# Expert outputs scattered back by token and loaded plainly, with expert tiles of two 256-row halves

## The reference

```
x = x + window_attention(group_norm(x))          # shifted 8x8 windows, 8 heads, relative bias
t = x as 32768 tokens of 128 channels
t = t + banded_attention(layer_norm(t))          # 128-token windows, 4 heads, band of 32
n = layer_norm(t)
probs = softmax(n @ gate_w + gate_b)             # 8 experts
top2_vals, top2_idx = top_k(probs, 2)
t = t + sum over the two chosen experts e of  top2_val * (gelu(n @ W1[e] + b1[e]) @ W2[e] + b2[e])
```

## Time and profile before

| | us |
|---|---|
| median of three runs | 3094.0 |
| the three runs | 3090.27 to 3098.82 |
| span of the profiled execution (first to last instruction) | 3088.7 |
| median over that span | 5.3 |
| PE busy | 2544.2 (82%) |
| VectorE busy | 1965.5 (64%) |
| POOL busy | 1914.2 (62%) |
| ACT busy | 1865.7 (60%) |

### The profile page before, as it was taken

How to read it: one execution, slowest core, us unless ns; L and a number is a source line. 1 busy time by engine, 2 the same in 40 slices (tenths; PEclk the granted TensorE clock), 3 DMA queues, 4 the chain that set the end, 5 groups by cost and what they waited for, 6 DMA issues and landing times.

```text
span 3088.7 us, 77036 instructions
## 1 busy us (share of the span) xinstructions
PE 2544.2 (82%) x27338; PEld 1794.8 (58%) x27338; DVE 1965.5 (64%) x5091; ACT 1865.7 (60%) x3409; POOL 1914.2 (62%) x2270
## 2 busy tenths in 40 slices
PE   6898889989888899889988988899888887676830
PEld 3565655556666666666666666666665665554520
DVE  4577777777666666777676676767776765522222
ACT  3666656666767677677776677767777654432310
POOL 1335555555444444576666576666667878779986
PEclk9998888888999999899999999999999988788965
DMA  5223333334445454144333343434343434456743
GB/s 208 104 110 117 117 132 150 147 127 138 147 173 182 161 183 161 60 148 123 100 122 117 107 144 122 126 96 127 119 149 111 131 109 135 123 171 203 244 127 91
DMA packets 262427, 421.99 MB, mean 137 GB/s; under 512 B 41740, under 2 KB 141080, under 8 KB 261280
## 3 DMA queue, kind: packets, MB, share of 16 engines
q1 hardware_dynamic: 219232, 327.69, 31.2%
q0 software_dynamic: 32768, 67.17, 7.7%
q10 hardware_dynamic: 10048, 22.19, 2.2%
HBM read 198.26 MB, written 231.22 MB: 139 GB/s over the span
## 4 chain that ended last, share of the span: by engine, by line
PE 48%; POOL 17%; ACT 15%; issue 10%; DVE 7%; DMA 2%; ACTq 1%; SPq 1%; POOLq 0%; DVEq 0%
PE bank_m L834 7%; POOL yg L1233 7%; PE bank_m L827 4%; PE bank_to L761 4%; POOL x_sorted L1223 4%; PE bank_s L801 4%; PE bank_s L807 3%; PE bank_s L716 3%; ACT pt_sb_a L1051 2%; POOL xin L1243 2%; PE bank_to L770 2%; PE bank_s L729 2%; ACT L1178 2%; ACT v_a L1036 2%; PE bank_s L739 2%
## 5 line engine op out<-in xcount | busy, mean ns | idle before, releaser
L1223 POOL DMA_INDIRECT x_sorted<-xn_c,place_i x512 | 534.3, 1044 | 282.1 <-PE bank_s L700 109.2
L1233 POOL DMA_INDIRECT yg<-y_sorted,place_i x512 | 521.4, 1018 | 241.1 <-PE bank_to L783 107.5
L1216 POOL TENSOR_TENSOR s_sb_a<-s_sb_a,mx_a 128x512 f32<-128x512 f32 x256 | 267.8, 1046 | 587.7 <-DVE mx_a L1607 586.9
L1599 DVE TENSOR_TENSOR s_sb_a<-bank_s,bias_a 128x512 f32<-128x512 f32 x256 | 176.6, 690 | 355.3 <-PE bank_s L700 257.7
L827 PE MATMUL bank_m<-xe,wk_e 128*128 128x512 f32 x552 | 280.5, 634 | 37.7 <-ACT hid L1084 27.7
L834 PE MATMUL bank_m<-wk_e,hid 128*128 128x128 f32 x2208 | 283.3, 291 | 0.9 <-ACT hid L1084 0.9
L834 PEld LDWEIGHTS bank_m<-wk_e,hid 128*128 128x128 f32 x2208 | 277.7, 208 | 2.2 <-issue 1.9
L1216 POOL TENSOR_TENSOR s_sb_b<-s_sb_b,mx_b 128x512 f32<-128x512 f32 x256 | 269.7, 1054 | 11.5 <-DVE mx_b L1607 11.5
L761 PE MATMUL bank_to<-k_consts,p_sb_b 128*128 128x128 f32 x1024 | 179.0, 300 | 92.2 <-ACT pt_sb_a L1051 56.1
L1051 ACT ACTIVATE pt_sb_b<-bank_to 128x512 f32<-128x512 f32 x256 | 152.5, 596 | 146.4 <-PE bank_to L761 145.7
L1207 POOL TENSOR_TENSOR km_a<-qk_a,k_consts 128x128 f32<-128x128 f32 x512 | 215.7, 445 | 40.0 <-DVE qk_a L1451 35.4
(11 more groups left out here) (221 smaller groups left out, 6266.7 us busy)
## 6 DMA issues: line engine op xcount, KB each, us to landing
y_sorted<-t_back SPq DMA_DIRECT2D x192, 512.0 KB, 5.5
y_sorted<-yo SPq DMA_DIRECT2D x170, 256.0 KB
wk_e<-in_w_experts_dram SPq DMA_DIRECT2D x134, 321.0 KB
xs<-x_sorted SPq DMA_DIRECT2D x134, 256.0 KB
t_kept<-t SPq DMA_DIRECT2D x64, 256.0 KB
t_back<-t_kept SPq DMA_DIRECT2D x32, 512.0 KB
xin<-in_x_dram SPq DMA_DIRECT2D x128, 112.0 KB
x_res<-in_x_dram SPq DMA_DIRECT2D x256, 56.0 KB
```

What stands on the lines that cost most here:

```text
L1216: pool.tensor_tensor(s[:, :, :], s[:, :, :], m[:, :, None].to_broadcast(shape), ALU.subtract).then_inc(s_sub[w], 1)
L1223: pool.indirect_dma_start(out=x_sorted[group_of[d] % XSIDES].ap(), out_offset=bass.IndirectOffsetOnAxis(ap=place_i[:, d, n:n + 1], axis=0) ...
L1233: pool.indirect_dma_start(out=yg[:, c % 2, n, :], out_offset=None, in_=y_sorted[side].ap(), in_offset=bass.IndirectOffsetOnAxis(ap=place_i ...
L1599: tt(s_sb[0][:, :, :].rearrange("p (r h) n -> p r (h n)", h=2), scores, bias_a[:, kind, :, :].rearrange("p (r h) n -> p r (h n)", h=2), AL ...
```

## The change

The order of moving rows is turned round. Before, outputs are stored sorted and gathered by token. Afterwards POOL scatters each output tile to its tokens' rows (`scatter_back`, four indirect DMAs of 128 rows for a tile, into `y_tokens`), and an image's outputs are then read with one plain 1 MB load on SP (`bring_back`). For that, each sorted token row carries two more numbers, its home row and its first expert (`ROW_W` is 130 instead of 128); DVE writes them in `gate_choices` (three more instructions for an image) and works the target row out in `slots_back` (two more for a tile). Spare places get rows with targets of their own (input `spare`).

A tile of 512 rows becomes two halves of 256 (`SLOTS = 256`, `PART = 2`), each with its own place and its own expert's weights: two row loads and two weight loads for a tile, each with its own values read from the table. `hidden` is four matmuls of 256 columns instead of two of 512, `gelu` four of 256 instead of two. The surplus of a group falls from 7 tiles of 512 to 8 of 256. `plan()` then gives 152 tiles in 76 pairs, all of two tiles: 57 pairs with 114 tiles in passes 10 to 31, 6 in passes 32 and 33, and 13 with 26 tiles in the tail, where images 22 to 31 are summed. Two images may be summed in a pass from pass 24 on; pass 16 has no pair, passes 15, 17, 22, 23 and 28 have two.

POOL's rows stand at places written out by hand: `OUT_AT` for the 16 scatters of an image, `BACK_AT` for the 8 rows of the pair in each slot, as (step, k) with steps 8 and up in the next pass. The memsets between rows, the fills with zeros, `store_pair` and `gather` go away. `yo` has three buffers, and DVE waits before it writes one until its four rows have landed.

```diff
-SLOTS = 512
+SLOTS = 256
+PART = 2
+ROOM = PART * SLOTS
+HOME, FIRST, ROW_W = D, D + 1, D + 2
+YO, MOVES = 3, PART * SUB
+BACK_AT = (((4, 1), (4, 1), (4, 2), (4, 3), (4, 3), (5, 0), (5, 1), (5, 2)),
+           ((6, 1), (6, 2), (6, 3), (7, 1), (7, 2), (7, 3), (8, 0), (8, 1)),
+           ((9, 1), (9, 2), (9, 3), (10, 1), (10, 2), (11, 0), (11, 1), (11, 2)))
+OUT_AT = ((5, 0), (5, 2), (5, 3), (6, 0), (6, 1), (6, 2), (6, 3), (7, 0), (7, 1), (7, 2), (7, 3),
+          (8, 0), (8, 1), (8, 2), (8, 2), (8, 3))
-TWO_SUMS_FROM = 29
-PAIRS_PER_SUM = 2.5
+TWO_SUMS_FROM = 24
+PAIRS_TO_SUM = 3
...
@@ load_pair @@
-                row = eng.value_load(tiles[0:1, kth:kth + 1], min_val=0, max_val=BUFFER - SLOTS)
-                expert = eng.value_load(tiles[0:1, MAX_TILES + kth:MAX_TILES + kth + 1], min_val=0, max_val=E - 1)
-                rows = x_sorted[side].ap()[bass.ds(row, SLOTS), :].rearrange("(p j) d -> p (j d)", p=P)
-                eng.dma_start(xs_b[b], rows).then_inc(tile_in[b], 16)
-                weights = w_experts[bass.ds(expert, 1), :, :].rearrange("e p n -> (e p) n")
-                eng.dma_start(wk_b[b], weights).then_inc(tile_in[b], 16)
+                for h in range(PART):
+                    at = kth + h
+                    row = eng.value_load(tiles[0:1, at:at + 1], min_val=0, max_val=BUFFER - SLOTS)
+                    expert = eng.value_load(tiles[0:1, MAX_TILES + at:MAX_TILES + at + 1], min_val=0, max_val=E - 1)
+                    rows = x_sorted[side].ap()[bass.ds(row, SLOTS), :].rearrange("(p j) d -> p (j d)", p=P)
+                    eng.dma_start(xs_b[b][:, h, :, :].rearrange("p j w -> p (j w)"), rows).then_inc(tile_in[b], 16)
+                    weights = w_experts[bass.ds(expert, 1), :, :].rearrange("e p n -> (e p) n")
+                    eng.dma_start(wk_b[b][:, h, :], weights).then_inc(tile_in[b], 16)
...
@@ bring_back @@
+                after(sp, stored[home], 16 * IO_DMAS * y_uses(c))
+                tiles_landed(sp, last_tile[group_of[c]])
+                first = last_image[group_of[c] - 1] + 1 if group_of[c] else 0
+                at = TOP * (SPARE + TOKENS * (c - first))
+                rows = y_tokens[group_of[c]].ap()[at:at + TOP * TOKENS, :]
+                sp.dma_start(y_home[home].rearrange("p t n d -> p (t n d)"),
+                             rows.rearrange("(p r) d -> p (r d)", p=P)).then_inc(y_in[home], 16)
...
@@ hidden @@
-                    mm(banks[:, ch, :], w[:, P * ch:P * ch + P], xe[:, m, :], start=True, stop=True).then_inc(z_ready, 1)
+                    for h in range(PART):
+                        own = slice(SLOTS * h, SLOTS * h + SLOTS)
+                        last = mm(banks[:, ch, own], w[:, h, P * ch:P * ch + P], xe[:, m, own], start=True, stop=True)
+                    last.then_inc(z_ready, 1)
...
@@ gelu @@
-                    func(hid[:, CH * m + ch, :], banks[:, ch, :], ACT.Gelu,
-                         bias=w[:, B1_AT + ch:B1_AT + ch + 1]).then_inc(gelu_ready, 1)
+                    for h in range(PART):
+                        own = slice(SLOTS * h, SLOTS * h + SLOTS)
+                        last = func(hid[:, CH * m + ch, own], banks[:, ch, own], ACT.Gelu,
+                                    bias=w[:, h, B1_AT + ch:B1_AT + ch + 1])
+                    last.then_inc(gelu_ready, 1)
...
@@ GpSimd @@
-            def gather(c, n):
...
-            def apart():
...
+            def scatter_back(u, k):
+
+                _, q, _ = pairs[u].members[k // MOVES]
+                if k % MOVES == 0:
+                    pool.wait_ge(yo_ready, q + 1)
+                j = k % MOVES
+                pool.indirect_dma_start(out=y_tokens[pairs[u].group].ap(),
+                                        out_offset=bass.IndirectOffsetOnAxis(ap=back_to[:, q % YO, j:j + 1], axis=0),
+                                        in_=yo[:, q % YO, j, :], in_offset=None).then_inc(y_out[q % YO], 16)
...
@@ slots_back @@
-                after(dve, y_out[q % 2], 16 * (q // 2))
-                tt(yo[:, q % 2, :, :], banks[:, m, :].rearrange("p (j d) -> p j d", j=SUB),
-                   w[:, None, B2_AT:B2_AT + D].to_broadcast([P, SUB, D]), ALU.add).then_inc(yo_ready, 1)
+                after(dve, y_out[q % YO], 16 * MOVES * (q // YO))
+                for h in range(PART):
+                    stt(back_to[:, q % YO, SUB * h:SUB * h + SUB], rows[:, h, :, FIRST], w[:, h, OWN_AT:OWN_AT + 1],
+                        rows[:, h, :, HOME], ALU.not_equal, ALU.add)
...
```

More of the change, by code:

```diff
@@ L119, in shape_constants @@
     put("base", rows(REGION * e))
+    put("experts", rows(e))
+    put("home", TOP * (SPARE + TILES * ch[:, None] + np.arange(TILES)[None]))
     img = np.zeros((SIDE, SIDE), np.int32)
@@ L171, in plan @@
     for g, size in enumerate(GROUPS):
-        tiles = list(range(TOP * size * TOKENS // SLOTS + E - 1))
+        tiles = list(range(0, TOP * size * TOKENS // SLOTS + SURPLUS, PART))
         for k in range(0, len(tiles), 2):
@@ L499, in load_residual @@
                                      x_rolled[a, r, c0:c1, tiles, :]).then_inc(xr_in[h], 16)
-            def store_pair(u):
-                pair = pairs[u]
-                side, tiles = pair.group % YSIDES, table[pair.group % TABLES]
-                if pair.group >= YSIDES:
-                    sp.wait_ge(summed, SUM_STEPS * (last_image[pair.group - YSIDES] + 1))
-                else:
-                    sp.wait_ge(filled[side], 16 * FILLS)
-                for m, q, kth in pair.members:
-                    sp.wait_ge(yo_ready, q + 1)
-                    row = sp.value_load(tiles[0:1, kth:kth + 1], min_val=0, max_val=BUFFER - SLOTS)
-                    rows = y_sorted[side].ap()[bass.ds(row, SLOTS), :].rearrange("(p j) d -> p (j d)", p=P)
-                    sp.dma_start(rows, yo[:, q % 2, :, :].rearrange("p j d -> p (j d)")).then_inc(y_out[q % 2], 16)
             def spill(c, h):
@@ L565, in _ @@
                     load_residual(a, 1)
-                if before[2] is not None:
-                    store_pair(before[2])
                 if here[1] is not None:
@@ L1300, in _ @@
                     step(i, t)
-            for k in range(12, TOP * TILES):
-                scatter(IMAGES - 1, k)
-                apart()
-            for c in sums[PASSES - 1][1:]:
-                for k in range(12, TOP * TILES):
-                    gather(c, k)
-                    apart()
-            for c in range(first_tail_sum, IMAGES):
-                for k in range(TOP * TILES):
-                    gather(c, k)
-                    if c < IMAGES - UNPAUSED:
-                        apart()
+            for row, (t, _) in enumerate(OUT_AT):
+                if t >= TILES:
+                    scatter(IMAGES - 1, row)
+            for u in tail:
+                for k in range(MOVES * len(pairs[u].members)):
+                    scatter_back(u, k)
         @block.vector
@@ L1540, in tile_table @@
                 if g >= TABLES:
-                    for n in range(2):
-                        dve.wait_ge(y_out[n], 16 * ((last_tile[g - TABLES] + 1 - n) // 2))
+                    dve.wait_ge(yo_ready, last_tile[g - TABLES])
                 tt(seen[:, :], total, const("base", 1), ALU.subtract).then_inc(tabled, 1)
```

326 lines of the change are left out of this document (161 added, 165 removed).

## The result

The changed kernel takes 3171.98 us (median of four runs, 3165.45 to 3175.18) against 3092.14 us for the kernel before on the same chip: 1.0265 times as long, 95% interval 1.0222 to 1.0307. The forecast was 3054 with a range up to 3140. It is slower, and outside the range. The profiled span is 3172.9.

What follows compares the result with a forecast made beforehand. PE was taken to set the pace in passes 18 to 28, POOL in pass 32 and the tail. Span 3088.7 + 113 (passes 10 to 31) - 16 (pass 32) - 137 (tail) = 3048.7, so 3054 measured; range 2935 to 3140.

Steps and rivals of the forecast that it cites:

- POOL's crowd in steps 6, 7 and 0: Passes 10 to 31: added scatter-back rows make POOL the bound there, +7.3 a pass, +5.8 without sums, +145 in all.
- Up to step 5 PE hides them: Three-pair passes: PE's work covers POOL's rows up to step 5, but for 0.7 by which step 6's subtraction comes late.
- the 6 forecast for `gelu`: Passes 10 to 31: four `gelu` of 256 columns cost 0 to 0.27 a tile, +6 for 114 tiles, bounds 0 and 31.
- slower rival: POOL sets the whole pass and PE's clock falls while it waits: 10.8 in each of 21 passes, 3136; chance 0.17.
- first rival: Rows hidden behind PE's chain, POOL's step 7 results ready before PE needs them: 0.7 a pass, 2924; chance 0.18.
- Halves: Expert tiles: `hidden` as four narrower matmuls costs 0, bounds -0.1 to +0.47 a tile; `gelu` +6 for 114 tiles.
- narrow matmuls: Rival: each of four more `hidden` records a tile costs a 128-column one, +66, giving 3120; chance 0.04.
- VectorE and SP: Added vector instructions cost 0, about 30 in all if uncovered; `slots_back` wait 0, or 1 to 2 a pass; SP's loads 0.
- Pass 32: 40 rows without memsets and 8 subtractions on POOL: 71 instead of 87.4, -16.
- The tail: No gather, 13 pairs instead of 20, ACT's rounds 13.4: 214 instead of 351.5, -137, bounds 175 and 285.
- the rival of late loads: Tail: twice the weights come late, pairs at 19 us, tail 285, total 3125; chance 0.09.
- The rule that speaks against rows on POOL: VectorE blocks GpSimd's DMA descriptors, 620 ns growing to 3100; 120 more rows caught would cost 470 us, judged not borne out.

Runs made afterwards that it cites:

- tail_sp: Changed kernel with the loads of the tail's pairs issued by SP instead of ACT; 3130.99 us, 1.0150 of the kernel before.
- tiles_512: Changed kernel with the halves undone: tiles of 512 rows with one place and one expert; 3171.35 us, 1.0279 of the kernel before.
- keys_first: Changed kernel, all 40 rows kept, two moved from between step 6's subtraction and masked keys to behind the keys; 3142.14 us, 1.0184 of the kernel before.
- gelu_whole: spread2 with `gelu` unsplit, two instructions of 512 columns a tile; 2993.02 us, 0.9695 of the kernel before.
- one_row_moved: Changed kernel scattering back one of a tile's four rows in the passes, slot 1's first moved behind step 6's masked keys; 2997.10 us, 0.9732 of the kernel before.
- spread2: Changed kernel, its 40 rows a pass spread over other places, none between step 6's subtraction and keys; 2996.76 us, 0.9723 of the kernel before.
- best: spread2's places with tail_sp's loads on SP, the tail's first two pairs' loads ahead of a store; 2951.59 us, 0.9564 of the kernel before.
- spread: Changed kernel with the same 40 rows a pass spread over other places, five in step 5; 3011.46 us, 0.9742 of the kernel before.

## Why the prediction was wrong, point by point

On the span, 3172.9 instead of 3048.7, it missed by 124: 72 in passes 10 to 31, 4 in pass 32 and 48 in the tail.

**POOL's crowd in steps 6, 7 and 0: right in mechanism, nearly right in size.** Subtraction to subtraction took 14.0 in step 6 (forecast 13.6) and 12.7 in step 7 (13.3); keys for step 1 were ready 5.5 after step 0's (5.2). From step 6's subtraction to step 1's scores it is 32.3, just the forecast without its 0.7. That subtraction came 1.5 late rather than 0.7 (4.52 after the scores, 3.00 before the change). Steps 6, 7 and 0 grew by 8.0 a pass (29.0 to 37.0); 7.3 was forecast.

**"Up to step 5 PE hides them": this step failed.** The sum ended at step 1's scores and put steps 1 to 5 at nothing; they grew by 3.1. Step 1 has 1.4 of it: PE now waits 2.2 for the keys before it, and in pass 24 its clock is 0.60 instead of 0.83. This goes with the crowd. In the four versions that have it (after, tail_sp, tiles_512, keys_first) the mean wait before step 1 is 1.5 to 2.2, its clock 0.63 to 0.66 and its length 12.0 to 12.4; in all others, before included, there is no wait, the clock is 0.76 to 0.89 and the length 9.9 to 11.0. Steps 2 and 4 have 0.6, from `gelu`. Step 3 has 1.1, which doesn't go with the crowd (11.9 in tiles_512, 12.9 in gelu_whole) and whose cause is open; in tail_sp, with the same passes, it has 0.5. The passes gained 11.1 instead of 7.3, and the six without sums 7.7 instead of 5.8 (85.2 to 93.0 in passes 11 to 14): 15 x 3.8 + 6 x 1.9 = 68. Less the 6 forecast for `gelu`, that is 62 of the 72 by which passes 10 to 31 missed. (By `plan()` passes 27 and 31 sum no image either, so the forecast's 15 passes at 7.3 should have been 13, 3 us less.) The text had this as its slower rival, POOL setting the pass and the clock falling with it, at 10.8 a pass; the passes went that way. The fault was to take waits and their clock for two cases, with chances of their own. one_row_moved shows that they come together: take the wait away, and the step after it is 1.0 shorter, at a clock of 1.00 instead of 0.86.

**The place of a row wasn't in the sum.** It counted rows per interval at 1.28 each, and 1.5 once for the slower keys. One row ahead of the keys of step 7 is worth some 48 us without the crowd; eighteen rows at other places cost nothing that can be measured (one_row_moved against spread2, 0.9732 and 0.9723). The rows had the sign: before the change PE already waited 0.83 for these keys in pass 24, so nothing put ahead of them could be hidden, and the first rival's "ready before PE needs them" doesn't hold for them. The rival that the rows would be hidden was right in what PE's chain can bear, and wrong about the places they were put at.

**Halves: the products right, `gelu` low.** A tile's eight matmuls take 1.97 to 1.99 (four took 1.95), 246 to 249 ns a record where half of 488 is 244: so about 0, and narrow matmuls are no cost. Four `gelu` took 1.57, above the 1.53 bound, and the rest wasn't "mostly beside PE's other work": steps 2 and 4 show 0.3 each. By tiles_512 halves cost 1.4 to 2.1 a pass, 26 to 40 in all, against 6 with a bound of 31; only 0.6 of it is traced to `gelu`, and most of the rest lies in step 3, whose time varies without them.

**VectorE and SP: right on the path, VectorE's work too low.** In passes 18 to 27 PE's waits that are put down to VectorE come to 8.0 us, where passes 18 to 28 before had 8.4, and one wait of 2.2 to a tile's weights. But "about 30 in all" for the added instructions, were they uncovered, was far too low: 284 of the new ones in `slots_back` (L1580) alone took 133.9, half of them about 0.22 or less each and the longest 2.76.

**Pass 32:** 75.1 instead of 71, so -12 for -16.

**The tail: mis-sized, 262.9 instead of 214.** The end was right in sum, 35.2 from the last tile's output at 3137.75 to the end, but three images are summed there, 4.7 each, where the text had one and slower loads. Three terms were low. The first pair's copy comes 17.5 after the tail's start instead of 4.5, since its loads stand behind a store in SP's list, and SP issues them until 2922.7. In best, where they stand ahead of that store, the copy comes 8 earlier (14.3 instead of 22.3 after ACT's last gating instruction).

```profile
2909.96 3.16 SPq L575 DMA_DIRECT2D out_dram<-yg  x8
2914.80 0.37 SPq L521 DMA_DIRECT2D qk_a<-x_sorted  x1
```

Rounds take 14.5 (3075.02 to 3089.52) instead of 13.4: about 12 over eleven. And twice the weights came late, 5.3 and 9.3 of ACT's idle time, as here on PE in the second case:

```profile
3044.26 1.09 PE L841 MATMUL bank_to<-k_consts,xs 128*128 128x128 f32 x4 [4.28 <-DMA wk_e<-in_w_experts_dram]
3048.91 1.12 PE L841 MATMUL bank_to<-k_consts,xs 128*128 128x128 f32 x4 [3.56 <-DMA wk_e<-in_w_experts_dram]
```

That is 13 + 12 + 15 = 40 of 48, the rest isn't traced; the rival of late loads came true in part, beside the slower rival and not in its stead. The range left out that both could happen.

**The rule that speaks against rows on POOL.** Of 1120 rows after, 49 took over 1.3 us, by 50 us in all over 1.0 each; before it was 68 of 1024 and 46. The Trainium skill (SBUF — State Buffer, "SBUF: two separate sides") has a DMA issued by GpSimd take some 620 ns alone and 3100 beside a VectorE copy. The trace agrees in a few rows, up to 3.07 us, and not in a price on every row, as the median row took 0.96. (The forecast's 470 us took 120 added rows; these counts make it 96.) Where VectorE's work reached PE's path in the steps read here, it was by POOL's masked keys, 2.26 beside its sums, not by the descriptors.

## What to carry to other kernels

On an engine that isn't full, ask of every added instruction what stands behind it in the list and who waits for that: one indirect DMA ahead of a small instruction that the matrix engine waits for cost some 48 us, eighteen at places with room nothing that could be measured. Work that has slack belongs in the stretch where the engine idles, here the end of step 3, and behind what is waited for. And price a wait of the matrix engine together with the lower clock that followed it in these runs: 2.75 us of wait brought 1.0 more in the next step.

## What the runs showed of the hardware that was not expected

After a wait of 3.59 us the first products of a pair's two tiles took 5.25 us, where they take 1.89 and 1.97 behind a wait of 0.83. POOL's masked keys took 0.76, 1.28 or 2.26 us according to what VectorE did beside them. Passes 5 to 9, without any expert work, averaged 70.3 to 71.7 us at a mean clock of 0.88 to 0.91 in the versions whose scatters stand at the places of the kernel before or after, and 68.2 to 69.6 at 0.95 to 0.97 in the five that moved scatters (keys_first, spread, spread2, gelu_whole, best). So the places of a pass's 16 scatters matter there too; which one, and why, wasn't tried.
